# Adapters' input products from each sample's own gathered columns instead of all eight adapters' columns

## What is computed

```python
def _lora_linear(x, W, A, B, adapter_indices):
    base = jnp.einsum('bsd,df->bsf', x, W)
    Ai = A[adapter_indices]
    Bi = B[adapter_indices]
    lora = jnp.einsum('bsr,brf->bsf', jnp.einsum('bsd,bdr->bsr', x, Ai), Bi)
    return base + lora
gate = _lora_linear(x, Wg, Ag, Bg, adapter_indices)
up = _lora_linear(x, Wu, Au, Bu, adapter_indices)
h = jax.nn.silu(gate) * up
x = x + _lora_linear(h, Wd, Ad, Bd, adapter_indices)
```

## Time and profile before

| | |
|---|---|
| median of 3 runs | 1266.41 us (1262.3 to 1268.48) |
| profiled execution, its own time | 1263.87 us |
| its span, first to last instruction | 1261.8 us |
| TensorE matmuls busy | 1249.3 us, 99% |
| VectorE busy | 977.8 us, 77% |
| GpSimd busy | 665.7 us, 53% |
| ScalarE busy | 559.2 us, 44% |
| chain that ended last | TensorE 90%, VectorE 5%, DMA 2% |

### The profile page before, as it was taken

The page is one execution under the profiler, slowest core; times in us unless marked ns, Lnnn a source line. Parts: engine busy times, 40 slices in busy tenths (PEclk is TensorE's granted clock), DMA queues, the critical chain, the costliest instruction groups (busy, mean ns, idle before and its releaser), DMA issues.

```text
span 1261.8 us, 17908 instructions
## 1 busy us (share of the span) xinstructions
PE 1249.3 (99%) x6204; PEld 1041.9 (83%) x6204; DVE 977.8 (77%) x1554; ACT 559.2 (44%) x993; POOL 665.7 (53%) x549
## 2 busy tenths in 40 slices
PE   8999999999999999999999999999999999999998
PEld 7788888888888888888888888888888888888886
DVE  6987777886788777788779768777888877777775
ACT  3744445444344444454444444444443434444432
POOL 4476555555635556545554556565555444445453
PEclk9999999999999999999999999999999999999999
DMA  5856345555965345445687444535477732243333
GB/s 193 299 177 221 121 119 166 159 146 170 378 203 189 105 122 150 128 131 175 218 316 218 158 126 147 153 120 136 146 289 267 229 93 89 70 117 101 118 92 109
DMA packets 141097, 210.11 MB, mean 167 GB/s; under 512 B 43473, under 2 KB 87761, under 8 KB 141009
## 3 DMA queue, kind: packets, MB, share of 16 engines
q1 hardware_dynamic: 118128, 137.03, 34.7%
q0 software_dynamic: 22016, 70.80, 17.0%
q10 hardware_dynamic: 864, 1.15, 0.2%
HBM read 164.89 MB, written 44.04 MB: 166 GB/s over the span
## 4 chain that ended last, share of the span: by engine, by line
PE 90%; DVE 5%; DMA 2%; issue 1%; ACT 1%; another core or an unknown queue 0%; SPq 0%; DVEq 0%; ACTq 0%
PE px L1544 28%; PE pd L1544 27%; PE py L1544 14%; PE pz L1544 7%; PE pz L1561 3%; PE pv L1590 2%; PE pv L1588 2%; PE pd L1822 2%; PE py L1561 2%; PE px L1561 1%; DVE wg_lo L1215 1%; DMA w_raw<-w_gu 1%; PE pd L1571 1%; PE pd L1665 0%; PE pd L1793 0%
## 5 line engine op out<-in xcount | busy, mean ns | idle before, releaser
L687 POOL TENSOR_TENSOR h_lo<-g,h_hi 128x512 fp32r<-128x512 f32 x127 | 184.3, 1451 | 336.2 <-ACT h_hi L809 335.5
L656 POOL DMA_INDIRECT b_got<-b_table,idx_b x192 | 197.5, 1029 | 58.5 <-issue 49.0
L1544 PE MATMUL px<-xo_hi,wg_hi 128*128 128x512 f32 x540 | 216.9, 402 | 2.1 <-ACT up L809 0.7
L1347 DVE TENSOR_TENSOR acc<-pd,acc 128x512 f32<-128x512 f32 x252 | 168.0, 686 | 63.0 <-PE pd L1544 59.9
L1215 DVE TENSOR_TENSOR wg_lo<-w_raw,wg_hi 128x512 fp32r<-128x512 f32 (+1 forms) x268 | 192.1, 720 | 31.1 <-issue 19.5
L1544 PE MATMUL px<-xo_hi,wg_lo 128*128 128x512 f32 x540 | 211.8, 392 | 0.0
L1544 PE MATMUL px<-xo_lo,wg_hi 128*128 128x512 f32 x540 | 210.4, 390 | 0.0
L809 ACT ACTIVATE wg_hi<-w_raw 128x512 fp32r<-128x512 f32 (+1 forms) x272 | 153.0, 570 | 114.9 <-PE py L1561 70.3
L1544 PE MATMUL pd<-wd_hi,h_hi 128*128 128x512 f32 x512 | 202.8, 396 | 0.0
L1544 PE MATMUL pd<-wd_lo,h_hi 128*128 128x512 f32 x512 | 201.0, 393 | 0.0
L1544 PE MATMUL pd<-wd_hi,h_lo 128*128 128x512 f32 x512 | 199.8, 390 | 0.0
(11 more groups left out here) (292 smaller groups left out, 2403.1 us busy)
## 6 DMA issues: line engine op xcount, KB each, us to landing
w_raw<-w_gu SPq DMA_DIRECT2D x68, 512.0 KB
wd_raw<-w_dn SPq DMA_DIRECT2D x64, 256.0 KB
xo_hi<-xops SPq DMA_DIRECT2D x21, 512.0 KB, 5.9
xo_lo<-xops SPq DMA_DIRECT2D x21, 512.0 KB, 6.9
acc<-x SPq DMA_DIRECT2D x8, 1024.0 KB, 8.4
ad_raw<-ad_table SPq DMA_DIRECT2D x16, 512.0 KB
xops<-st_hi SPq DMA_DIRECT2D x24, 256.0 KB, 2.7
xops<-st_lo SPq DMA_DIRECT2D x24, 256.0 KB, 2.9
```

What stands on the lines that cost most here:

```text
L656: gp.indirect_dma_start(out=dst, out_offset=None, in_=rows_of, in_offset=bass.IndirectOffsetOnAxis(ap=rows.bitcast(U32), axis=0)).then_inc ...
L687: return gp.tensor_tensor(dst, src_raw, src_hi, ALU.subtract)
L1347: ins = dve.tensor_tensor(dst, pd[j][:, :], dst, ALU.add)
L1544: ins = pe.matmul(psum, w_parts[wi], x_parts[xi], start=(start and i == 0), stop=(stop and i == 2), skip_group_check=more)
```

## The change

In quarters 1 to 3 the adapters' unit no longer multiplies by the columns of all adapters. For each of a quarter's 16 samples GpSimd gathers the sample's own 16 gate and 16 up columns (`gather_own`: 128 rows of 512 bytes each, into `st_lo`). Four samples' columns make one 128-column weight, which meets only those four samples' 256 tokens: `own_products`, 2 x 2 x 2 x 3 = 24 matmuls of 256 columns for each half, 48 a quarter, into `py` (t = 0) and `px` (t = 1). The plain operands A11, A12 and S1, A22 are used. S1 is A21 + A22, so the weights of its partner are made by `own_difference`.

- The splits are `weights_high` and `weights_low` of four groups of 512 columns in the slots of the input weights (group 3 in `u`). `c11`, `u3`, `c12`, the `keep_` copies and `sums` of that unit go, and two of four `ua_high` and `ua_low`.
- The result's rows are already ordered by sample, so the selectors are the same for all samples: `sel_own` is made once, by 12 ScalarE copies in quarter 0's block 14, and all six later `selectors` go. Small tiles now lie in `f_one`.
- Gathers: samples 0 to 4 at the end of block 13, 5 and 6 and then 7 to 11 in block 14, 12 to 15 in block 15 ahead of `h_low(15, 0)`. The four `ad_rows` gathers of a boundary move behind: two to the end of block 15, two into the adapters' unit, their first stores into that unit too. `gather_bd(q, 0)` goes ahead of the second `gather_b` of block 15.
- SP: no weights are loaded for that unit; block 0's are loaded in its place, in block 14. The tokens come in the order A11, S1, A12, A22, S2, S3, S4.
- Two more index operations in `half_numbers` and one in `gather_numbers`.

Counts of the semaphores change with it. The core of the diff:

```diff
+            def gather_own(q, samples):
+                for s in samples:
+                    home = flat(st_lo[:, :, :])[:, s * P:(s + 1) * P]
+                    gather_rows(home, a_in_rows, idx_own[:, (q - 1) * QS + s:(q - 1) * QS + s + 1], own_got[s // (2 * TP)])
...
@@ GpSimd, in its loop @@
                 if b == -1:
                     if q:
                         gp.wait_ge(bdown_mm, (q - 1) * QP + TP)
                         gather_bd(q - 1, 1)
+                        for g in range(2, AD_GROUPS):
+                            gather_ad(q, g)
                     continue
...
                 if b % 2:
-                    gp.wait_ge(c11_done, n)
+                    gp.wait_ge(c11_done, k)
                     ad_low(q, b // 2)
...
+                if to_own and b == BLOCKS - 1:
+                    gather_own(q + 1, range(12, 16))
...
                     h_low(q, b, 0)
...
-                if b == BLOCKS - 2 and q + 1 < QUARTERS:
-                    for g in range(2, AD_GROUPS):
-                        gather_ad(q + 1, g)
+                if to_own and b == BLOCKS - 2:
+                    gather_own(q + 1, range(5, 7))
...
                 if b == BLOCKS - 3 and q + 1 < QUARTERS:
                     for half in range(2):
                         gp.wait_ge(xops_out[half], TP * (q + 1) * 64)
+                    gather_own(q + 1, range(0, 5))
+                if to_own and b == BLOCKS - 2:
+                    gather_own(q + 1, range(7, 12))
+                if to_own and b == BLOCKS - 1:
+                    for g in range(4):
+                        gp.wait_ge(w_done[g], n + 2)
                     for g in range(2):
                         gather_ad(q + 1, g)
...
@@ ScalarE, weights_high(n, g) @@
+                if n % UNITS == 0:
+                    if g < 3:
+                        act.wait_ge(own_got[g // 2], n // UNITS * 2 * TP * 16)
+                    else:
+                        act.wait_ge(own_diff, n // UNITS)
+                    src, hi_part, _ = own_group(g)
+                    copy(hi_part, src).then_inc(w_hi_done[g], 1)
+                    return
...
@@ ScalarE, in its loop @@
                 if b == -1:
                     v_lower(q - 1, 0)
                     v_high(q - 1, 0)
+                    weights_high(n, 3)
                     v_lower(q - 1, 1)
+                    ua_high(q, 0)
+                    weights_high(n + 1, 0)
+                    weights_high(n + 1, 1)
+                    weights_high(n + 1, 3)
+                    ua_high(q, 1)
+                    v_high(q - 1, 1)
+                    weights_high(n + 1, 2)
+                    continue
...
+                if (q, b) == (0, BLOCKS - 2):
+                    act.wait_ge(sel_mm, 2)
+                    act.wait_ge(slots_done, 1)
+                    for m in range(2):
+                        for s in range(HS + 2):
...
                 copy(h_hi[:, 1, b % 2, :], g1[:, :]).then_inc(h_hi_done[1], 1)
+                if to_own:
+                    weights_high(n + 1, 2)
...
@@ VectorE, in its loop @@
                 if b == -1:
-                    v_low(q - 1, 0)
-                    c11(n)
-                    u3(n)
-                    ua_low(q, 0, 0)
-                    c12(n)
-                    ua_low(q, 1, 1)
-                    ua_low(q, 0, 1)
                     sums(n + 1)
+                    ua_low(q, 0)
                     weights_low(n + 1, 0)
-                    ua_low(q, 1, 0)
+                    weights_low(n + 1, 1)
+                    finish(q - 1, 0, (0,))
+
+                    ua_low(q, 1)
+                    finish(q - 1, 0, (1,))
 
                     select(q, 0)
-                    weights_low(n + 1, 1)
+                    finish(q - 1, 0, (2, 3))
                     weights_low(n + 1, 2)
-                    finish(q - 1, 0)
                     weights_low(n + 1, 3)
-                    selectors(q, 1)
                     continue
...
                 for phase_at in down_phases(q, b):
                     add_down(*phase_at)
...
-                if b == BLOCKS - 1 and q + 1 < QUARTERS:
-                    selectors(q + 1, 0)
+                    if to_own and not phase_at[2]:
+                        v_low(q, 0)
+                        own_difference(q + 1)
+                        weights_low(n + 1, 2)
+                        weights_low(n + 1, 3)
...
@@ TensorE @@
+            def own_products(q, t):
+                for cp in range(2):
+                    k = ((A11, A12), (S1, A22))[t][cp]
+                    tokens_ready(q, k)
+                    pe.wait_ge(w_done[2 * t + cp], unit(q, -1) + 1)
+                    w_parts = own_homes(2 * t + cp)
+                    for c in range(2):
+                        for a in range(2):
+                            cols = slice((2 * c + a) * P, (2 * c + a + 1) * P)
+                            tok = slice(c * TOK + a * HALF, c * TOK + (a + 1) * HALF)
+                            for i, (wi, xi) in enumerate(((0, 0), (0, 1), (1, 0))):
+                                ins = pe.matmul(ua_bank(q, t, 0)[:, a * HALF:(a + 1) * HALF], w_parts[wi][:, cols],
+                                                (xo_hi, xo_lo)[xi][:, k, tok], start=(cp == c == a == i == 0),
+                                                stop=True, skip_group_check=True)
+                ins.then_inc(own_mm, 1)
...
+                if b == -1:
+                    pe.wait_ge(c12_done, k)
+                    own_products(q, 0)
+                    pe.wait_ge(c21_kept, k)
+                    own_products(q, 1)
+                    pe.wait_ge(down_add, 5 * q * 2 * SUPER)
+                    finish(q - 1, 0)
+                    pe.wait_ge(c22_done, k)
+                    select(q, 0)
+                    continue
```

More of the change, by code:

```diff
@@ L315, in cond_resid_kernel @@
         down_add = sem("down_add")
+        own_got = [sem(f"own_got{t}") for t in range(2)]
+        own_diff = sem("own_diff")
+        own_mm = sem("own_mm")
+        slots_done = sem("slots_done")
         ua_hi_done = sem("ua_hi_done")
@@ L577, in _ @@
                 n = unit(q, b)
+                k_done = blocks_done(q, b)
+                if b == -1 and q:
+                    for g in range(2):
+                        store_ad(q, g)
+                if b >= 0 and b % AD_BLOCKS == 0 and n > 1:
+                    load_ad(q, b // AD_BLOCKS)
                 if b == 0 and q:
@@ L941, in _ @@
                     ad_high(q, b // 2)
+                k = blocks_done(q, b)
+                to_own = b == BLOCKS - 1 and not last
                 if b == -1:
@@ L1041, in _ @@
                     keep_c21()
-                act.wait_ge(p3_mm, n)
-                if not last and b > 1:
+                act.wait_ge(p3_mm, k)
+                if not last and not to_own and b > 1:
                     weights_high(n + 1, 2)
@@ L1059, in _ @@
                     weights_high(n + 1, 2)
-                if not last:
+                if not last and not to_own:
                     weights_high(n + 1, 3)
@@ L1370, in finish, with own_difference, ua_low @@
                     dve.tensor_tensor(dst, finish_bank(q, t, j)[:, :], dst, ALU.add).then_inc(y_add, 1)
-            def ua_low(q, t, m):
-                src = ((g0, up0), (g1, up1))[t][m] if q else first_banks[t][m]
-                dve.wait_ge(ua_hi_done, 4 * q + ua_order(q, t, m))
-                dve.tensor_tensor(h_lo[:, t, m, :], src[:, :], h_hi[:, t, m, :], ALU.subtract).then_inc(ua_done, 1)
+            def own_difference(q):
+                dve.wait_ge(own_got[1], q * 2 * TP * 16)
+                first, last_two = (own(cp)[:, 2 * TP:QS, :, :] for cp in range(2))
+                dve.tensor_tensor(last_two, last_two, first, ALU.subtract).then_inc(own_diff, 1)
+            def ua_low(q, t, m=0):
+                dve.wait_ge(ua_hi_done, ua_made(q, t, m))
+                dve.tensor_tensor(h_lo[:, t, m, :], ua_bank(q, t, m)[:, :], h_hi[:, t, m, :], ALU.subtract).then_inc(ua_done, 1)
             def c11(n):
@@ L1492, in _ @@
                     half_numbers()
-                if not last and not late:
+                if (q, b) == (0, BLOCKS - 3):
+                    dve.wait_ge(layer_mm, QP)
+                    dve.tensor_copy(pattern_kept, pattern)
+                    for at in range(2 * HS):
+                        ins = dve.tensor_scalar(slot_mask[:, at:at + 1], p_f[:, 0:1], float(at), None, ALU.is_equal)
+                    ins.then_inc(slots_done, 1)
+                if not last and not late and not to_own:
                     sums(n + 1)
@@ L1506, in _ @@
                                       ).then_inc(f_done, 1)
-                c11(n)
+                c11(k)
+                if to_own:
+                    weights_low(n + 1, 0)
                 behind = parts_at(q, b) is not None
@@ L1515, in _ @@
                     token_low(q, parts_at(q, b))
-                c12(n)
+                c12(k)
                 gate0()
```

310 lines of the change are left out of this document (161 added, 149 removed).

## The result

| | changed | before | ratio, 95% interval |
|---|---|---|---|
| first comparison, chip A, 17 runs each | 1270.24 us | 1263.77 us | 1.0047 [1.0039, 1.0054] |
| chip D (12 and 34 runs) | 1262.63 | 1263.30 | 0.9991 [0.998, 1.0002] |
| chip E (10 and 25) | 1262.78 | 1263.39 | 0.9995 [0.9984, 1.0006] |
| chip F (10 and 27) | 1263.49 | 1263.06 | 0.9998 [0.9985, 1.0011] |

The forecast was 1.9 us less (0.9985); its 1264.5 was counted from 1266.41, the median of three runs of the kernel before, where 17 have 1263.77. The first comparison gave 6.5 more between the medians. On three other chips the same kernel was, by the ratios, 1.1, 0.6 and 0.3 us faster than before, 0.7 on the mean. The profiled execution of A has a span of 1268.7 us, 6.9 over that of before.

The account below looks back on a forecast made before the run. TensorE was taken as the bound, busy 1249.3 of 1261.8 us. A boundary: -3.8 - 0.4 + 2.5 + 0.6 = -1.1; three make -3.3, plus 1.4 once: -1.9, so 1264.5 us, range 1255 to 1274.

Parts of the forecast that it names:

- The products: Adapters' unit on TensorE: 48 products of 256 columns at 0.12, 5.8 us, replace 42 of 512, 9.61; 3.8 saved a boundary.
- GpSimd: Blocks 14 and 15: sixteen gathers instead of four make `h_low(15,0)` late for TensorE; 2.5 us lost a boundary, bounds 2.0 and 3.6.
- VectorE's chain before block 0: VectorE's operations after `h_low(15,0)`, up to `ua_low(q,1)`, end after block 0's first product wants them; stall 0.6 us (0 to 1.8).
- Moves at no cost: Boundary: moved `ad_rows` gathers and stores, weight and token loads and `gather_bd` cost nothing; H is TensorE's resumption at `h_low(15,0)`.
- Block 0: Block 0 after a boundary: VectorE loses `selectors` and weights load earlier, so 0.4 of 0.77 us lost there comes back.
- Once in quarter 0: Block 14 of quarter 0: twelve ScalarE copies for `sel_own` cost 1.1 us; with added index operations 1.4 (0 to 2.5).
- The clock rival: A 2.5 us stand drops TensorE's clock to 1.2 GHz; 2.7 us a boundary makes it 0.5% slower; chance 0.08.

Follow-up runs that it names:

- `u3` first: Changed kernel with `u3` ahead of `weights_low` of groups 0 and 1 on VectorE in block 15; chip B, ratio 1.0051 to the kernel before.
- token order run: Changed kernel with block 15's token loads in the old order (A11, S1, S2, A12, S3, S4, A22); chip B, ratio 1.0047 to the kernel before.
- halves in turn: Changed kernel with each pass of the unit's 48 products made for both 256-column halves alternately; ratio to the kernel before 1.0003 on C, 1.0001 on E.
- one stop: Changed kernel with `stop=True` only on the last of each 24 unit products; ratio to the kernel before 0.9997 on C, 0.9998 on D, 0.9999 on F.

## Why the prediction was wrong on one chip and near on three

1. **The products**, -3.8 a boundary. Right where counts are prompt, and at A's first boundary: 48 starts 0.12 apart, 347.12 to 352.75, 5.75 us against 5.8. At A's third they stretch from 964.33 to 971.38, 1.4 more.
2. **GpSimd**, +2.5. The mechanism is right to its order: `h_low(15, 0)` directly behind the fourth gather, `u3` held behind `weights_low`, one stall and not two (experiment `u3` first). The size is 1.75 to 1.9, under the lower bound of 2.0.
3. **VectorE's chain before block 0**, +0.6. On D, E and F the way to block 0 has 9.52 - 8.94 = 0.58 of waits, but not these: `select` and block 0 follow `finish` at once in most. 0.52 of the 0.58 stands ahead of `finish`, mostly on the landing of the `bd` gathers.
4. **"Moves at no cost: `gather_bd(q,0)` starts by H + 5 and is needed at H + 15.4."** It starts at H + 5.1 on D (337.46, H at 332.35) and is needed at H + 16.0. What failed is that it was taken as landed: its last gather is issued by 342.4 and `finish` starts at 349.07, 6.7 us later, in a stretch with the DMA engines at 1.03 of their time. In the trace of before, the same gather went out at 343.08 to 344.7 and `finish` at 350.35 did not wait: it had landed 5.1 us after its issue, on D it took 6.5. The token order was named there as costless; it moved S2 to S4 into this stretch. That it is what made the landing later is likely, not shown (the token order run).
5. **Block 0**, -0.4. Wrong: 14.74 to 14.80 at all twelve boundaries of the changed kernel for 14.82.
6. **Once in quarter 0**, +1.4. The copies cost 0.86 (1.1 said), shown by moving them. The rest of quarter 0 differs more from profile to profile of one kernel (block 15's fifth product starts at 322.35, 323.01, 323.44 on D, E, F and 327.05 on A, with the clock at half twice in A's first 65 us) than the terms to be found.
7. **The clock rival.** Given 0.08 with stands of over 2.5 us in mind. It did come, after stands of 1.8, in some boundaries; where it came it took about 1.6 us, not 2.7 or more a boundary. Even so it is what leaves 0.7 of some 2.6 us on the three prompt chips. By the rule cited for it (the Trainium skill, "TensorE: Matmul & The Clock Gate", section "HAM oscillation — how this bites in real kernels"), idle gaps re-throttle the clock; the rows of chip F agree, and those of D and E, with the same stand and a clock of 1.00, show that not every one does.

From block 15's fifth product to block 0's start took 30.85, 30.80 and 30.84 us before. On D, E and F it is 30.03 on the mean of nine, -0.80; the forecast's terms for this way (-3.8 + 2.5 + 0.6) are -0.7. The sum was near by two errors that offset: 0.7 too much for the stall, and 0.6 missing in what is left, 0.35 of it the clock (twice 1.6 in nine boundaries), the rest not placed.

**The step that failed on chip A** is in the sum under "VectorE's chain": it has 0.1 for a hand-over, the unit's results among them, and so puts the lateness of a count at nothing, for products in a row of 48 at 0.12. There it takes 2.4 to 5.5, `ua_high` and all behind it are late, block 0 starts 4.0 us after the increment (4.7 where it is 2.35 late), and a boundary is 31.46 on the mean, +0.6 where -0.7 was forecast. None of the rivals had this. The size on A has a second part that no term had: the 3.5 us lost in quarter 0 of its profile beside the copies, with the clock at half twice. What makes the counts late stays open. It came on two of six chips, all 17 executions on A being slower than all 32 on D, E and F (1267.56 and more against 1266.03 and less), but each chip had one occasion, and on the same two a quarter of the semaphore records is missing. That it takes a run of small products is only seen, at this place and at the start, and not tested on such a chip. Whether halves in turn, one stop or a shorter row would avoid it there stays open: every run of these fell on prompt chips. Each execution here has a recorded span and clock; none without the recording stands beside them. The Trainium skill ("NOTIFIC — the notification-queue block", section "7.1 Overflow: three behaviours, one of which stalls the engine") says that the block which takes the records holds its producers back when its inner pipeline is full; no run here shows whether that is what delays the counts, or whether they would be late without the recording.

## What to carry to other kernels

Before explaining a difference of half a per cent, run the unchanged kernel once more beside the experiments: here three unlike edits all looked like cures until the control was as fast. Then sort the runs by their mean granted clock: a gain can be that of fewer drops. When many small products replace fewer large ones, the pitch of their starts is not yet the time at which another engine gets the result; look in the trace of before for a result after a row of small products that comes "remote" and late, and put work between such a row and its consumer. Where a transfer is moved in a queue, sum the bytes in flight in the stretch that it is moved into, not only the time at which it is needed.

## What was not expected of the hardware

- On two of six chips, each used once, the increment of the first 24 in a row of 48 products of 256 columns came 2.4 to 5.6 us behind the recorded start; on four, 0.29 to 0.30. Where counts were placed on each three products, they came 1.43 us apart, and 0.05 apart at the end. On such a chip two products near the end of the row started up to 1.2 us apart, with no input missing. The kernel before was as fast on the late chips (1263.8, 1262.9) as on the prompt ones (1263.0 to 1263.4).
- A stand of TensorE of 1.8 us was followed in some executions by 3.4 us at the lower clock, and in others, with the same stand, by none.
- Two VectorE operations with both inputs in SBUF took 3.77 us where they met three of GpSimd's tensor operations, and 2.45 with one placed before them on the same queue.
